# A Mamba block with attention on one core: in the column scans the remainder gets a PSUM bank and a Y tile of its own, and VectorE adds the two Y in the mix stage

## The reference, cut to what matters

```python
x_hw = xc.reshape(Bsz, D, L)                              # row order
x_wh = xc.transpose(0, 1, 3, 2).reshape(Bsz, D, L)        # column order
xs = jnp.stack([x_hw, x_wh, x_hw[..., ::-1], x_wh[..., ::-1]], axis=1)
x_dbl = jnp.einsum('kcd,bkdl->bkcl', x_proj_w, xs)
dts, Bv, Cv = jnp.split(x_dbl, [R, R + N], axis=2)        # R = 12, N = 4 states
dt = jax.nn.softplus(jnp.einsum('kdr,bkrl->bkdl', dt_proj_w, dts) + dt_proj_b[None, :, :, None])
ys = _selective_scan(xs, dt, A, Bv, Cv) + Ds[None, :, :, None] * xs   # h = exp(dt*A)*h + dt*B*u ; y = sum_n h*C
y = ys[:, 0] + ys[:, 2, :, ::-1] + (ys[:, 1] and ys[:, 3, :, ::-1], put back from column order)
y = _ln_cf(y, out_norm_w, out_norm_b) * silu(z)
out = x + jnp.einsum('cd,bdhw->bchw', out_proj_w, y)
```

## Time and profile before

| what | value |
|---|---|
| median of 3 runs | 9575.38 us (9568.02 to 9575.95) |
| the profiled execution | 9585.77 us, span 9583.9 us |
| PE / DVE / ACT / POOL busy, share of the span | 92 / 76 / 65 / 34 % |
| scan's column half, image 0 | 422 to 649 us |
| mix, image 0 | 655 to 779 us |

### The profile page before, as it was taken

The page is one execution under the profiler, slowest core; times in us unless marked ns, Lnnn a source line. Parts: engine busy times, 40 slices in busy tenths (PEclk is TensorE's granted clock), DMA queues, the critical chain, the costliest instruction groups (busy, mean ns, idle before and its releaser), DMA issues. The chain is left out here.

```text
span 9583.9 us, 104556 instructions
## 1 busy us (share of the span) xinstructions
PE 8813.6 (92%) x26564; PEld 4729.1 (49%) x26564; DVE 7318.6 (76%) x8161; ACT 6190.6 (65%) x7500; POOL 3294.3 (34%) x1874
## 2 busy tenths in 40 slices
PE   7899988999889998899988999889998899989999
PEld 3336733367333673336733367333673336633366
DVE  6977769777697767977679776797767977679776
ACT  6765667656676566755667656675566755677555
POOL 2860028500385003850038500385003850048400
PEclk9999999999999999999999999999999999999999
DMA  1320013200132002320013200132002320023200
GB/s 52 114 77 12 11 54 112 72 12 11 54 114 72 11 10 61 109 71 11 12 59 113 68 10 12 59 114 67 10 12 63 110 67 10 12 66 114 60 11 12
DMA packets 286701, 503.35 MB, mean 53 GB/s; under 512 B 142155, under 2 KB 143215, under 8 KB 253431
## 3 DMA queue, kind: packets, MB, share of 16 engines
q1 hardware_dynamic: 286199, 497.81, 17.4%
HBM read 467.99 MB, written 29.47 MB: 52 GB/s over the span
## 5 line engine op out<-in xcount | busy, mean ns | idle before, releaser
L1313 DVE TENSOR_TENSOR pl<-pf,ph 128x1024 fp32r<-128x1024 f32 x1024 | 1254.6, 1225 | 1014.1 <-ACT ph L961 1006.3
L1175 DVE TENSOR_TENSOR_SCAN h<-ps,h,dbu 128x512 f32<-128x512 f32 x1536 | 1886.8, 1268 | 65.9 <-POOL dbu L1026 29.9
L1026 POOL TENSOR_TENSOR dbu<-bs,du 128x1024 f32<-128x1024 f32 x768 | 1800.9, 2375 | 54.1 <-POOL du L1017 54.1
L961 ACT ACTIVATE ph<-pf 128x1024 fp32r<-128x1024 f32 x1024 | 1086.5, 1061 | 753.0 <-PE ps L652 752.7
L955 ACT ACTIVATE pf<-ps 128x1024 f32<-128x1024 f32 x1024 | 1051.5, 1027 | 534.9 <-PE ps L639 534.9
L981 POOL MEMSET sqb<- 64x512 f32 x16 | 8.3, 520 | 3998.1 <-issue 3993.2
L824 ACT ACTIVATE ps<-dt,negA 128x512 f32<-128x512 f32 x1536 | 1038.3, 688 | 494.5 <-DVE h L1175 494.1
L1297 DVE TENSOR_REDUCE mx<-ps 128x1 f32<-128x512 f32 x1792 | 1168.9, 684 | 78.4 <-PE ps L557 60.4
L1183 DVE TENSOR_TENSOR hc<-h,ps 128x1024 f32<-128x1024 f32 x768 | 938.0, 1221 | 194.9 <-PE ps L478 113.5
L478 PE MATMUL ps<-xhl,selr 128*128 128x512 f32 x1536 | 847.8, 639 | 147.7 <-DVE hc L1183 147.5
L1011 POOL TENSOR_TENSOR dt<-dt,ze 128x1024 f32<-128x1024 f32 x256 | 605.9, 2367 | 923.7 <-ACT dt L817 923.5
(11 more groups left out here) (191 smaller groups left out, 14691.2 us busy)
## 6 DMA issues: line engine op xcount, KB each, us to landing
bs<-rows SPq DMA_DIRECT2D x256, 1024.0 KB, 5.2
bs<-rows SPq DMA_DIRECT2D x512, 256.0 KB, 6.1
xa<-in_x SPq DMA_DIRECT2D x130, 256.0 KB, 2.9
xb<-in_x SPq DMA_DIRECT2D x130, 128.0 KB, 3.0
out<-fa SPq DMA_DIRECT2D x64, 256.0 KB, 2.1
rdb<-rden SPq DMA_DIRECT2D x56, 192.0 KB, 3.4
out<-fa SPq DMA_DIRECT2D x64, 128.0 KB, 2.4
xhl<-ct SPq DMA_DIRECT2D x256, 8.0 KB
```

Source lines behind the costliest of these rows:

```text
L961: A(ph[:, mp % 2, :, :], pf[:, mp % 2, :, :], ACT.Copy).then_inc(S["ph_ready"], 1)
L1026: pool.tensor_tensor(dbu[:, q, :, :], bs[par][:, q, :, :], du[:, r:r + 1, :].to_broadcast([P, 2, T]), ALU.mult).then_inc(S["dbu_ready"], 1)
L1175: dve.tensor_tensor_scan(h[:, j, ::step], ps[:, 2 + e, ::step], dbu[:, q, e, ::step], h[:, j, end:end + 1], ALU.mult, ALU.add)\
L1313: TT(pl[:, mp % 2, :, :], pf[:, mp % 2, :, :], ph[:, mp % 2, :, :].bitcast(F32), ALU.subtract)\
```

## The change

In the column steps the remainder's sum moves from bank 1 to bank 0 (free there, since the row steps' x projection is over). For direction 1 it starts from nothing and ACT stores it into a new tile `ycol`, in the order of the columns; for direction 3 PE reads `ycol` back (`old_rest_col`). The rows' remainder stays in `gate[:, 1]`. PE's order in a column step becomes: spread 1, dtproj, old Y0, spread 2, product 0, (old rest), next step's spread 0, products 1, and the fold of product 2, which stood in the next step before. `add_y0` moves into the next step, ahead of `add_y1`. `xsf` is cut to the 64 partitions that are used, since `ycol` lies in the other 64 of the same memory. In the mix, `copy_rem` on ACT goes away; VectorE's `add_rem` adds `gate` and `ycol` (read across the columns) into `yt`, twice ahead of the loop, and for chunk c + 2 at the end of step c.

```diff
             xsf = sb("xsf", [P, L], where=at_pad1)
+        with ExitStack() as at_pad1:
+            ycol = sb("ycol", [P, L], where=at_pad1)
         pad1 = sb("pad1", [P, PW * PW])
...
     pe.wait_ge(S["dt_ready"], g + 1)
-    src = xd[:, :] if at < EV else xsf[:, c * T:(c + 1) * T]
+    hi = P if at < EV else R
+    src = xd[:, :] if at < EV else xsf[0:R, c * T:(c + 1) * T]
     for r in range(2):
-        m = mm(ps[:, 6 + r, :], wdt[:, (2 * k + r) * P:(2 * k + r + 1) * P], src, start=True, stop=True)
+        m = mm(ps[:, 6 + r, :], wdt[0:hi, (2 * k + r) * P:(2 * k + r + 1) * P], src, start=True, stop=True)
     m.then_inc(S["dtpre_ready"], 1)
...
+def old_col(c, g):
+    pe.wait_ge(S["y1_added" if g is None else "y0_added"], b * G + (EV + 1) if g is None else g + 1)
+    mm(flat(ps[:, 1, :]), eye[:, :], chunk(pad0, c, 1), start=True, stop=False)
+def add_col(g):
+    pe.wait_ge(S["hc_ready"], g * NP + 4)
+    for e in range(2):
+        m = mm(ps[:, 1, :], eye[:, :], hc[:, 0, e, :], start=False, stop=False)
+    m.then_inc(S["summed"], 1)
+def old_rest_col(c, g):
+    pe.wait_ge(S["y1_added"], g + 1)
+    mm(ps[:, 0, :], eye1[R:P, :], ycol[R:P, c * T:(c + 1) * T], start=True, stop=False)
+def rest_col(k, g):
+    if k == 1:
+        pe.wait_ge(S["y1_added"], g + 1)
+    pe.wait_ge(S["hc_ready"], g * NP + 6)
+    for e in range(2):
+        m = mm(ps[:, 0, :], foldw[:, :], hc[:, 2, e, :], start=(k == 1 and e == 0), stop=(e == 1))
+    m.then_inc(S["summed"], 1)
 def sum_second(g):
...
 def body(at, par, g, before, now, nxt, after):
+    if at >= EV:
+        if at == EV:
+            sum_rest(*before, g - 1)
+            pe.wait_ge(S["xlo_ready"], b * EV + (EV + 1))
+        spread(1, *now, at, g)
+        if after:
+            dtproj(*after, at + 2, g + 2)
+        old_col(now[1], None if at == EV else g)
+        spread(2, *now, at, g)
+        add_col(g)
+        if now[0] == 3:
+            old_rest_col(now[1], g)
+        if nxt:
+            spread(0, *nxt, at + 1, g + 1)
+        sum_second(g)
+        rest_col(now[0], g)
+        return
     if after and at + 2 < EV:
...
 run_chunks(pe, b, body)
-sum_rest(K - 1, 0, g_0 + G - 1)
 barrier(pe, b, 0)
...
-    A(chunk(xsf, c, 1), flat(ps[:, 0, :]), ACT.Identity, bias=eye[:, ONE:ONE + 1]).then_inc(S["xs_ready"], 1)
+    A(chunk(xsf, c, 1, 0, R), flat(ps[0:R, 0, :]), ACT.Identity, bias=eye[0:R, ONE:ONE + 1]).then_inc(S["xs_ready"], 1)
...
     act.wait_ge(S["summed"], g * NP + 6)
-    A(chunk(gate[:, 1], c, k % 2, R, P), flat(ps[R:P, 1, :]), ACT.Copy).then_inc(S["y1_added"], 1)
+    if k % 2:
+        A(ycol[R:P, c * T:(c + 1) * T], ps[R:P, 0, :], ACT.Copy).then_inc(S["y1_added"], 1)
+    else:
+        A(chunk(gate[:, 1], c, 0, R, P), flat(ps[R:P, 1, :]), ACT.Copy).then_inc(S["y1_added"], 1)
...
     if before:
+        if at > EV:
+            add_y0(*before, g - 1)
         add_y1(*before, g - 1)
...
         decay(nxt[0], 0, 1, s + 3, 1 - par, g + 1)
-    add_y0(*now, g)
+    if at < EV:
+        add_y0(*now, g)
 g_0 = b * G
...
 run_chunks(act, b, body)
+add_y0(K - 1, 0, g_0 + G - 1)
 add_y1(K - 1, 0, g_0 + G - 1)
...
     A(thc[par][0][0:O, :], thf[:, :], ACT.Copy).then_inc(S["thh_ready"], 1)
-def copy_rem(c, q):
-    A(yt[0:R, q, :], gate[R:P, 1, bass.ds(c * T, T)], ACT.Copy).then_inc(S["yt_ready"], 1)
...
         A(phh[0:O, bass.ds(c * T, T)], phf[:, :], ACT.Copy).then_inc(S["phh_ready"], 1)
-        if not isinstance(c, int) or c + 2 < NCH:
-            copy_rem(c + 2, par)
         act.wait_ge(S["gt_ready"], i + 1)
...
             split_theta(i, 0)
-copy_rem(0, 0)
-copy_rem(1, 1)
 run_mix(act, step)
...
 dve.memset(mx[:, :, 0:1], -3.0e38).then_inc(S["mx_link"], 1)
+def add_rem(c, q):
+    TT(flat(yt[0:R, q, :]), flat(gate[R:P, 1, bass.ds(c * T, T)]), chunk(ycol, c, 1, R, P), ALU.add)\
+        .then_inc(S["yt_ready"], 1)
...
             low_theta(i, 0)
+        if not isinstance(c, int) or c + 2 < NCH:
+            add_rem(c + 2, par)
+add_rem(0, 0)
+add_rem(1, 1)
 run_mix(dve, step)
```

## The result

The changed kernel took 9773.2 us (median of 4 runs, 9768.91 to 9778.58) against 9573.59 of the kernel before: ratio 1.021, interval 1.0192 to 1.0227. It is slower by 2.1%, 15 us from the forecast of 9758 and inside its range.

The account below looks back on a forecast made before the run. Bounds: in column steps two equal loops, VectorE with PE and POOL's; in the mix, PE. Terms -38 - 24 + 174 + 71 = +183 us on the median 9575.38 gave 9758 us, range 9670 to 9840.

Parts of the forecast that it names:

- the step that decides: In the mix, PE's mean waits for VectorE's add at the end of the step before; steps of 15.2 us against 11.67.
- The chain: In the mix, mean to join to add to next mean, 3.55 us more a step; 174 us in eight images.
- The add: VectorE's `add_rem` in the mix, priced at 1.05 us, between 0.67 and 1.29.
- The clock: In the mix, PE's standstill brings a clock fall in each gated step, 1.47 us each, 71 us in all.
- Rival 1: In the mix, the mean is gated but the clock holds, or a fall hides; sum +112, 9687 us; chance 0.17.
- Rival 2: In the mix, each clock fall lasts through more of the step and costs twice; +254, 9829 us; chance 0.10.
- The column half: Column steps gain 38 us until POOL's loop bounds them, the end of the half 24; together 62 us gained.
- rival 3: No gain in the column half, since PE's new order puts a new wait there; +245, 9820 us; chance 0.07.
- Rival 4: In the mix, the add doesn't hold the mean, only its own time counts; -31, 9544 us; chance 0.06.

## Why the prediction was right

*The direction and the step that decides.* "PE's step c + 1 begins with the mean of chunk c + 2 and its wait for that add": shown by the trace, and by the two kernels that move it. With the clock held the means are 15.1 us apart, where the sum had 15.2. The chain was put at 174 us and measured 159 (the mix of the kernel with PE kept busy, less the mix before).

*The add.* Taken at 1.05 us between 0.67 and 1.29; measured 1.01 at the median of the 64. The Trainium skill ("Vector Engine (DVE) Microarchitecture Reference", 5.2 Measured stream behaviour on trn2) has its 1.73 ns per column for hops of 4 KiB, and the estimate from it was 0.96 us; here the hops are of 256 bytes, and the measurement lies 6% above the estimate.

*The clock.* Six falls per image were expected; the changed kernel's mixes have 8 stretches at 1.2 GHz each, the mixes before 2 or 3, and 2 again with PE kept busy. The falls were priced at 1.47 us from the column steps, 71 us; keeping PE busy gave back 94, 1.95 each. This is the largest error of the sum. Image 0's mix, changed and then with PE kept busy:

```profile
646.20:803.16 156.96, 122.17 (x348) 61.41 (x349) 81.87 (x132) 46.90 (x79) 11.14 (x10) 0.84 0.08 25
```

```profile
647.11:791.34 144.23, 124.96 (x384) 63.51 (x385) 81.87 (x132) 46.88 (x79) 11.13 (x10) 0.93 0.10 28
```

Over the eight images the mixes spend 378 us at 1.2 GHz, and 156 with PE kept busy: 4.6 us per gated step. The fall from which the price was taken is 12 us at 0.86, 3.4 us at 1.2 GHz. So the falls in the mix are longer by about a third, and so is their price. That some of a fall hides in a column step and none in the mix may add to it; this was not tested. Rival 1 (the clock holds) is out. Rival 2 (each fall lasts through more of the step) was right in kind, but its price, twice 71, is far above the 94 measured.

Around the standstills the granted clock is 0.85, and with three matmuls in each it is 1.00 (676 to 710 us). The Trainium skill ("TensorE: Matmul & The Clock Gate", What's actually happening) has the rule that activity releases the throttle, and the trace agrees.

*The column half.* Forecast -62, measured -32.1 and -17.9. That POOL's loop takes over is shown by its idle (22.5 against the 22.7 that the prediction had as the floor), by the wait at softplus, and by the pair of kernels with the shorter product. So rival 3 (no gain) is out. The term was some 12 us too large, and the error lies in the last step. The fifteen steps before it gained 42.0, where the loops were to give 38; the stretch behind the last product gained 17.9, where 16 were expected. But in the last step the sum took VectorE's wait for the spread, 1.00 us, as gone (-8 us in eight images), and the step got 9.9 us longer: the waits at products 0 and 1 are 1.1 to 2.0 and 0.7 to 1.6 us, after a fall of the clock. How long they are goes with the fall: two of the eight images of the version with the add in the gap have a shorter one, wait 0.3 and 0.7 us there, and have last steps of 12.0 us, as before. No kernel was made to hold the clock in that place.

*Rival 4, faster, by an add that ends before PE needs it,* is what the version with the add in the gap does: -62 us by its median against the shared runs of the kernel before, where the rival had -31 for an add that still cost its own time. The condition given for it (some 3.5 us earlier) agrees: the add in the gap ends at 689.64, 6.4 us ahead of the mean that needs it. Where between the two places the loss sets in was not tested.

*The total* is nearer than its terms. In the profiled executions the clock was 23 us above its term, the chain 15 below, the column half gained 12 less, and stretches that the sum put at nothing were 10 us shorter; together that is 10. The 10 us of the other stretches are spread over the projection, the rows' half and attention, which differ by as much between the kernels of the experiments. That the errors cancel is luck; the mechanisms do not rest on it.

## What to carry to other kernels

When an operation moves to another engine, look at where in that engine's queue it stands, and who waits for it: an operation of 1 us that was made in the middle of a step cost 3.3 us (5.3 with the clock) at the end of one, and nothing in a gap ahead of a wait. Before counting a wait as a gain, look for a second loop of the same length: here POOL's, readable as a chain of rows without idle. A standstill of PE in every step cost, here, the delay of the chain and the slow matmuls that followed it (159 and 94 us). And look at the last step of a loop by itself: what bounds the others need not bound it.

## What was not expected of the hardware

TensorE's clock falls more often in the column half after the change, and ahead of the last step no cost of it shows. These are the same 215 us of image 0, 418 to 633, first before, then after, then with the old matmul kept:

```profile
418.00:633.00 215.00, 200.69 (x387) 74.31 (x386) 195.74 (x167) 159.73 (x194) 184.50 (x91) 0.97 0.34 105
```

```profile
418.00:633.00 215.00, 197.16 (x373) 71.43 (x374) 200.47 (x170) 152.66 (x194) 188.03 (x92) 0.91 0.34 105
```

```profile
418.00:633.00 215.00, 203.92 (x390) 73.49 (x389) 200.92 (x170) 154.11 (x196) 188.66 (x92) 0.94 0.34 105
```

PE has less to do and is granted less: 0.97, then 0.91. Each step now has several short waits instead of one of 0.84 or 0.91 us:

```profile
507.06 1.11 PE L481 MATMUL ps<-xhl,selr 128*128 128x512 f32 x2 [0.23 <-DVE hc L1225]
508.88 1.98 PE L468 MATMUL ps<-xsf,wdt 64*128 64x512 f32 x4 [0.71 <-DVE dt L1207]
```

The matmuls are slower, but VectorE, which waits for POOL, does not see it. With the one matmul back PE is granted 0.94; the first fourteen steps of the eight images take 1575 us, and 1574 without it (0.91 in image 0). Only the last step, where VectorE no longer waits for POOL, shows the fall. So in these runs a low granted clock on PE cost time where PE was on the chain, and none that shows elsewhere.
